# Spreading the scan input of a Mamba layer over its states: one fp32 product on 32 rows instead of three stacked bf16 parts

## The chip, the cores and the metric

One NeuronCore of a Trainium2 chip runs the whole program in one launch. The time is device microseconds (us) of that core, from a run without a profile; the profile comes from one more execution. Engines: TensorE (PE), VectorE (DVE), ScalarE (ACT), GpSimd (POOL) and SyncE (SP), which here only issues DMAs.

## What is computed

Two layers over eight sequences of 512 tokens with 128 features. The first layer (attention between 16 heads, a feed-forward part and a normalisation, plus the routing for the second layer's experts) is not touched. The second layer is a Mamba block beside a mixture of experts. Its heart, for each sequence, with 256 channels d and 16 states n:

```
u  = silu(conv(x @ in_proj));  dt = softplus(dt_r @ dt_proj + b);  A = -exp(A_log)
h[d,n](t) = exp(dt[d](t) * A[d,n]) * h[d,n](t-1)  +  dt[d](t) * u[d](t) * B[n](t)
y[d](t)   = sum over n of h[d,n](t) * C[n](t)
out = (y + u*D) * silu(z) @ out_proj,   added to the experts' result and the residual
```

All of it is fp32 in the reference.

## The kernel before

`layer0` runs first, then `layer1`; the change is in `layer1`. There the eight sequences are "batches" b = 1 to 8, and a batch has 32 groups k: a group holds 8 channels by 16 states, one pair on each of the 128 partitions, over 512 time steps. The table `order` gives for group k the channel half s (k // 16), then i, then j, with j the fastest; SEG is 16, the groups of one half.

For each group:

- `spread_du` (TensorE, L1839) copies dt\*u of the 8 channels to the 128 partitions of the group by a product with a 0/1 matrix `spread`. The result is in one of two PSUM buffers `p_du`. It waits until the scan two groups back has released the buffer.
- `inject` (VectorE, L1726) multiplies `p_du` by the repeated B in place.
- `decay` (ScalarE, L1607) makes exp(dt\*A) in place in the tile `decays` (two of its four buffers lie in `slots`), three groups ahead; a DMA (`load_decays`) has brought dt repeated over the states from the DRAM scratch `dt_rows`, one load for each four groups.
- `scan` (VectorE, L1733) is the recurrence over the 512 steps, into one of four buffers `hs`.
- `times_c` (GpSimd, L1471) multiplies by the repeated C, into `hc`.
- `gather_y` (TensorE, L1848) sums over the states, once for four groups: four fp32 products, each into 32 output columns.

The orders are written out by hand: `batch()` of each engine lists what it does at each k, and each engine executes its list in order. TensorE at step k starts with `spread_du(b, k + 1)` and then does what falls due: the projections of the batch after next (`project_u` at k = 22 to 25 with two taps each, `project_z` at 27 and 29), those of the next batch (`x_proj` at 8, `dt_proj` at 10 and 12), `gather_y` at 2, 6, 10 and so on, `out_proj` at 6 and 23, and the experts. A plan has ten expert units for each batch, two of the shared expert and eight tiles of 256 tokens (48 tiles in all, so batches 7 and 8 have none of their own), due at step 10 + 3.2 m for m = 0 to 9. `due(b, k, ahead)` gives the units to be started: the turn of the tile 7 steps ahead, its gate 6, its up 5, its down product at the due step. VectorE has the unit's `half` (L1746) 4 steps ahead, `skip` at 3 and 19, `result` at 8, and the two ends of the softplus (`softplus_cut`, `softplus_end`, L1705 and L1710) at 15 and 16. GpSimd has the expert product `hidden` (L1483), `steps` at 17 and 19, `gate_y`, and from batch 4 on 64 indirect DMAs that fetch expert results (`fetch`, L1507).

The value that is spread has to be exact to fp32. The kernel before gets this with three bf16 parts. `steps` (GpSimd, L1459 and L1463) makes dt and then dt\*u in the tile `dtu`. For each half s of the next batch: ScalarE rounds dt\*u to bf16 (`first_part`, L1594), VectorE subtracts it (`second_rest`, L1715), ScalarE rounds the rest (`second_part`, L1598), VectorE subtracts again (`third_part`, L1720). They stand at k = 19 to 26. Each part is moved by four DMAs of SyncE's queue (`stack`, L1329, at k = 21 to 23 and 25 to 27) from partitions 32c..32c+31 to rows 32i..32i+31 of the tile `block_in`, so that one bf16 product over 96 rows adds the three parts. SyncE's list also holds the loads of expert weights (`wm`, L1309) and rows (`xg`, L1300), and those of the decays (L1358), and it waits in order.

Before batch 1 a prologue does the same for the first batch: dt\*u, parts, stacks, then the loop.

A fp32 product shows in the trace as two matmul instructions, each with a weight load of its own; a bf16 product as one. So L1848 has 512 instructions and L1839 has 256.

Of the kernel before, what the change touches and what calls it, by code (L numbers as in the profile page):

```python
# [17 lines left out]
BF16 = mybir.dt.bfloat16  # L18
# [43 lines left out]
def constants():  # L62
# [11 lines left out]
    spread = np.zeros((3, 32, 4, 128), np.float32)  # L74
# [20 lines left out]
    for i in range(2):  # L95
# [8 lines left out]
        "c_spread": spread.reshape(96, 4, 128),  # L104
# [1007 lines left out]
def layer1(nc, outer, io, moe, out, ident, w_loaded, n_loads, ready1, hold, w):  # L1112
    with ExitStack() as ctx:
# [13 lines left out]
        NB = 3  # L1127
# [4 lines left out]
        spread = sb("spread", [96, 4, 128], BF16)  # L1132
# [14 lines left out]
        dtu = sb("dtu", [128, 2, ST, T])  # L1147
        ez, rz = dtu[:, 0], dtu[:, 1]
# [3 lines left out]
        rest = wz  # L1152
        part = sb("y_part", [128, ST, 3, T], BF16)

        block_in = sb("block_in", [96, NB, 4, T], BF16)
# [41 lines left out]
        part1 = count("y_part1", 2)  # L1197
        rest1 = count("y_rest1", 2)
        part2 = count("y_part2", 2)
        part3 = count("y_part3", 2)  # L1200
        stacked = [count(f"y_stacked{i}", 3 * 4, 16) for i in range(ST)]
# [73 lines left out]
        def _(sp):  # L1275
            start(sp, [*xt_in, *ht_in, bc_out, bc_in, *stacked, *dt_out, *decays_in, *wm_in, *xg_in, *os_out])
# [41 lines left out]
            def stack(b, s, i):  # L1318
                made = (part1, part2, part3)[i]
                if i == 0:  # L1320
                    if s:
                        sp.wait_ge(du_full.sem, du_full.at(b - 1, SEG))
                    else:
                        sp.wait_ge(du_full.sem, du_full.at(b - 2))
                    hold(sp)
                sp.wait_ge(made.sem, made.at(b, s + 1))
                hold(sp)
                for c in range(4):
                    sp.dma_start(block_in[32 * i:32 * i + 32, (2 * b + s) % NB, c], part[32 * c:32 * c + 32, s, i]).then_inc(stacked[s].sem, 16)  # L1329

            def store_dt(b, s):
# [5 lines left out]
                sp.dma_start(dt_d[b % 2, s].rearrange("r (j t) -> j r t", j=4), dtu[:, 0, s]).then_inc(dt_out[s].sem, 16)  # L1337
# [49 lines left out]
            def prologue():  # L1387
                load_ht(1)
                sp.dma_start(hs[0:96, 2], io["c_spread"].rearrange("r i c -> r (i c)")).then_inc(staged, 16)
# [623 lines left out]
```

## Time and profile before

| | us |
|---|---|
| runs without a profile (3) | 1251.82, 1258.43, 1283.87; median 1258.43 |
| profiled execution, its time | 1268.29 |
| profiled execution, its span | 1266.5 |
| TensorE busy with matmuls | 856.6 (68%) |
| VectorE busy | 934.0 (74%) |
| GpSimd busy | 722.6 (57%) |
| ScalarE busy | 509.3 (40%) |
| first and last scan of layer 1 start at | 544.0 and 1247.3 |
| mean granted TensorE clock | 0.813 of full speed |

The shares of busy time are means over two different layers. The first layer ends at about 500 us; the scans fill the stretch from 544 us to the end but for the last 20 us. The times of runs without a profile scatter by 2.5% here, more than their distance to the profiled execution.

### The profile page before, as it was taken

The page shows a single profiled execution, that of the slowest core. Times are in us where ns is not written, and L with a number is a line of the kernel's source. Part 1 is how long each engine was busy: PE and PEld are TensorE (multiplying, and loading weights), DVE is VectorE, ACT ScalarE, POOL GpSimd, SP SyncE. Part 2 cuts the span into 40 slices and gives each one's busy share as a digit, 9 for nine tenths or more (in the row PEclk, how much of TensorE's full clock was granted, in tenths as well). Part 3 has the DMA queues.
Part 4 walks back from the last instruction along what each step waited for, and adds up shares of the span by engine and source line. Part 5 has one row for each costly group of instructions (what it writes and reads, how often), then busy time and mean ns, then how long its engine had stood idle before and what let it go on. Part 6 is the DMA issues. An engine that isn't in the chain of part 4 may idle for free. (4 is left out here: it accounts for less than half of the span.)

```text
span 1266.5 us, 13006 instructions
## 1 busy us (share of the span) xinstructions
PE 856.6 (68%) x3620; PEld 407.2 (32%) x3620; DVE 934.0 (74%) x1280; ACT 509.3 (40%) x842; POOL 722.6 (57%) x555
## 2 busy tenths in 40 slices
PE   3667888878855717347887878757778777834543
PEld 1123333333322312114544435424444444411210
DVE  3567887798785540176898798859989898969773
ACT  1012312322211103246576585664684574742330
POOL 1022112112106517455778677749998898679996
PEclk9668978998958757767998988978999888955755
DMA  4986666664702123366675766765776777645641
GB/s 126 217 176 154 152 173 174 152 182 109 160 32 83 59 93 121 84 160 198 162 216 178 180 215 167 198 188 125 182 206 162 189 207 173 204 119 112 135 121 29
DMA packets 102835, 192.32 MB, mean 152 GB/s; under 512 B 13131, under 2 KB 68108, under 8 KB 90348
## 3 DMA queue, kind: packets, MB, share of 16 engines
q1 hardware_dynamic: 91500, 183.07, 54.2%
q0 software_dynamic: 11264, 8.43, 3.8%
q8 instruction: 29, 0.48, 0.2%
q14 instruction: 42, 0.34, 0.1%
HBM read 146.80 MB, written 32.06 MB: 141 GB/s over the span
## 5 line engine op out<-in xcount | busy, mean ns | idle before, releaser
L1471 POOL TENSOR_TENSOR hc<-hs,c_rep 128x512 f32<-128x512 f32 x256 | 377.4, 1591 | 114.1 <-DVE hs L1733 113.7
L1726 DVE TENSOR_TENSOR p_du<-p_du,b_rep 128x512 f32<-128x512 f32 x256 | 175.2, 684 | 62.4 <-PE p_du L1839 62.0
L1839 PE MATMUL p_du<-block_in,spread 96*128 96x512 bf16 x256 | 111.4, 441 | 126.8 <-DVE hs L1733 119.5
L1733 DVE TENSOR_TENSOR_SCAN hs<-slots,p_du 128x512 f32<-128x512 f32 x128 | 156.2, 1220 | 40.6 <-POOL hc L1471 27.0
L1733 DVE TENSOR_TENSOR_SCAN hs<-decays,p_du 128x512 f32<-128x512 f32 x128 | 156.2, 1220 | 14.0 <-POOL hc L1471 3.0
L1507 POOL DMA_INDIRECT y_xr<-moe_sums,position x64 | 108.5, 1696 | 39.2 <-issue 25.1
L447 POOL TENSOR_TENSOR sc<-ex,ex_part 128x1024 f32<-128x1024 f32 x8 | 17.0, 2127 | 187.3 <-ACT ex_part L546 187.3
L682 DVE TENSOR_TENSOR value_prod<-p_eb,v 128x512 f32<-128x512 f32 x128 | 83.6, 684 | 37.4 <-PE p_eb L963 37.1
L1607 ACT ACTIVATE decays<-decays,a_neg 128x512 f32<-128x512 f32 x128 | 87.7, 716 | 49.5 <-DMA decays<-dt_rows 49.2
L1848 PE MATMUL p_y<-hc,gather 128*32 128x512 f32 x512 | 83.7, 732 | 35.0 <-POOL hc L1471 35.0
L1839 PEld LDWEIGHTS p_du<-block_in,spread 96*128 96x128 bf16 x256 | 25.4, 100 | 246.2 <-DVE hs L1733 200.8
L1483 POOL TENSOR_TENSOR y_hid<-y_hid,g_in 128x512 f32<-128x512 f32 x64 | 98.3, 1536 | 2.3 <-DVE y_hid L1746 2.3
L1607 ACT ACTIVATE slots<-slots,a_neg 128x512 f32<-128x512 f32 x128 | 89.7, 723 | 24.4 <-DMA slots<-dt_rows 24.4
L1811 PE MATMUL y_misc<-y_ht,wtap 128*128 128x512 f32 x128 | 74.3, 716 | 36.2 <-ACT ur L1550 20.7
L1868 PE MATMUL p_g<-xgt,wm 128*128 128x256 f32 x192 | 61.3, 448 | 47.1 <-ACT xgt L1613 28.6
L1619 ACT ACTIVATE g_in<-p_g 128x512 f32<-128x512 f32 x64 | 38.1, 595 | 112.3 <-PE p_g L1868 87.5
L658 DVE TENSOR_TENSOR score_prod<-qb,p_k 128x2048 f32<-128x2048 f32 x32 | 72.4, 2282 | 12.4 <-issue 6.9
L1895 PEld LDWEIGHTS p_o<-wm,y_hid 128*128 128x128 f32 x384 | 59.5, 225 | 12.7 <-issue 10.8
L1895 PE MATMUL p_o<-wm,y_hid 128*128 128x128 f32 x384 | 59.6, 307 | 0.9 <-ACT os L1626 0.9
L1868 PEld LDWEIGHTS p_g<-xgt,wm 128*128 128x128 f32 x192 | 39.5, 220 | 60.7 <-issue 35.1
L927 PE MATMUL p_s<-score_prod,sum_d 128*32 128x512 f32 x256 | 46.3, 805 | 17.4 <-DVE score_prod L658 17.4
L464 POOL TENSOR_TENSOR root<-var,half 128x8 f32<-128x8 f32 x8 | 13.2, 1648 | 73.2 <-DVE var L731 73.2
(184 smaller groups left out, 1666.2 us busy)
## 6 DMA issues: line engine op xcount, KB each, us to landing
qb<-rq_rows SPq DMA_DIRECT2D x32, 1024.0 KB, 14.1
decays<-dt_rows SPq DMA_DIRECT2D x32, 1024.0 KB
slots<-dt_rows SPq DMA_DIRECT2D x32, 1024.0 KB
wm<-in_wmoe SPq DMA_DIRECT2D x48, 384.0 KB, 13.8
moe_rows<-zeros SPq DMA_DIRECT2D x8, 774.0 KB, 6.3
xg<-moe_rows SPq DMA_DIRECT2D x48, 129.0 KB, 13.7
stack<-ex_part SPq DMA_DIRECT2D x96, 64.0 KB
block_in<-y_part SPq DMA_DIRECT2D x192, 32.0 KB, 5.8
```

The lines of the kernel that those rows point to most:

```text
L682: nc.vector.tensor_tensor(value_prod[:, n % NP], p_eb[:, n % 2], v[:, b % NV], ALU.mult).then_inc(weighed.sem, 1)
L1471: nc.gpsimd.tensor_tensor(hc[:, k % NA], hs[:, k % 4], c_rep[:, p], ALU.mult).then_inc(hc_done.sem, 1)
L1483: nc.gpsimd.tensor_tensor(hid[:, v % 2], hid[:, v % 2], g_in[:, v % 2], ALU.mult).then_inc(hid_done.sem, 1)
L1507: nc.gpsimd.indirect_dma_start(xr[:, b - 1, t], None, moe["sums"][grp], bass.IndirectOffsetOnAxis(ap=position[:, grp, kk, TT * i + t:TT * ...
L1607: nc.scalar.activation(decay_of, decay_of, ACT.Exp, scale=a_neg[:, g:g + 1]).then_inc(da_done.sem, 1)
L1726: nc.vector.tensor_tensor(p_du[:, k % 2], p_du[:, k % 2], b_rep[:, p], ALU.mult).then_inc(dbu_done.sem, 1)
L1733: nc.vector.tensor_tensor_scan(hs[:, k % 4], decays[(8 * (b - 1) + k // 4) % NQ][:, bass.ts(j, T)], p_du[:, k % 2], 0.0, ALU.mult, ALU.add ...
L1811: ins = nc.tensor.matmul(p_misc[:], wtap[:, k, bass.ts(n, 128)], ht[:, b % 2, k:k + T], start=(k == 0), stop=(k == CONV - 1))
L1839: nc.tensor.matmul(p_du[:, k % 2], spread[:, i], block_in[:, (2 * b + s) % NB, j], start=True, stop=True).then_inc(du_full.sem, 1)
L1848: ins = nc.tensor.matmul(p_y[32 * j:32 * j + 32], w["gather"][:, i], hc[:, k % NA], start=(i == 0), stop=(i == 3))
L1868: ins = nc.tensor.matmul(p_g[:, bass.ts(f, 256)], wm[:, j % NR, bass.ts(f, 128)], xgt[:, j % 2], start=True, stop=True)
L1895: ins = nc.tensor.matmul(p_o[:, bass.ts(i, 128)], hid[:, v % 2, 256 * f + 128 * i:256 * f + 128 * i + 128], wm[:, j % NR, 2 * FF1 + 128 * ...
```

## The change

The three parts, their stacks, the tiles `y_part` and `block_in` and all their semaphores go. `spread` becomes an fp32 matrix that stands four times, once for each block of 32 partitions, and TensorE multiplies the 32 partitions of the block j of dt\*u, where they lie, by it. `dtu` is split into `dt`, `rz` and a double-buffered `du`, so that dt\*u of the next batch can stand beside that of this one.

```diff
-        spread = sb("spread", [96, 4, 128], BF16)
+        spread = sb("spread", [128, 4, 128])
-        dtu = sb("dtu", [128, 2, ST, T])
-        ez, rz = dtu[:, 0], dtu[:, 1]
+        dt = sb("dt", [128, ST, T])
+        du = sb("du", [128, 2, ST, T])
+        rz = sb("rz", [128, ST, T])
+        ez = dt[:]
-        part = sb("y_part", [128, ST, 3, T], BF16)
-        block_in = sb("block_in", [96, NB, 4, T], BF16)
...
             def spread_du(b, k):
                 s, j, i = order[k]
                 if k % SEG == 0:
-                    pe.wait_ge(stacked[s].sem, stacked[s].at(b))
+                    pe.wait_ge(dt_step.sem, dt_step.at(b, 2 * s + 2))
                 pe.wait_ge(scanned.sem, ...)
-                nc.tensor.matmul(p_du[:, k % 2], spread[:, i], block_in[:, (2 * b + s) % NB, j], start=True, stop=True)
+                nc.tensor.matmul(p_du[:, k % 2], spread[32 * j:32 * j + 32, i], du[32 * j:32 * j + 32, (b - 1) % 2, s], start=True, stop=True)
...
-                nc.gpsimd.tensor_tensor(dtu[:, 1, s], dtu[:, 0, s], u[:, p, s], ALU.mult)
+                    pool.wait_ge(du_full.sem, du_full.at(b - 2))
+                nc.gpsimd.tensor_tensor(du[:, p, s], dt[:, s], u[:, p, s], ALU.mult)
...
-            def stack(b, s, i):             # SyncE
-            def first_part(b, s):           # ScalarE, L1594
-            def second_part(b, s):          # ScalarE, L1598
-            def second_rest(b, s):          # VectorE, L1715
-            def third_part(b, s):           # VectorE, L1720
...
             # SyncE, prologue
-                load_decays(1, 0)
-                for i in range(3):
-                    stack(1, 0, i)
-                for q in (1, 2):
+                for q in range(3):
                     load_decays(1, q)
-                for i in range(3):
-                    stack(1, 1, i)
```

The waits on `part3` in `dt_in` and `one_more` become one wait on `dt_step`. In the prologue the load of `spread` goes straight into its tile, without the conversion to bf16 on VectorE (L1698). Everything else, and the place of every other step, stays.

## Rows read from the trace of the kernel before

**Rows 1.** Stretches from first scan to first scan of batches 1 to 8, all engines.
```profile
544.00:634.30 90.30, 66.74 (x264) 35.43 (x265) 70.77 (x81) 52.63 (x91) 59.49 (x46) 0.81 0.68 177
634.30:719.80 85.50, 66.57 (x308) 38.35 (x307) 72.56 (x83) 55.12 (x99) 63.20 (x49) 0.92 0.68 189
719.80:804.90 85.10, 67.77 (x310) 39.26 (x309) 72.71 (x83) 55.34 (x100) 63.25 (x49) 0.90 0.68 190
804.90:903.10 98.20, 68.04 (x314) 38.85 (x313) 82.57 (x84) 55.46 (x100) 74.40 (x57) 0.90 0.66 169
903.10:994.90 91.80, 69.67 (x307) 39.99 (x306) 80.08 (x83) 55.41 (x99) 82.78 (x62) 0.89 0.72 184
994.90:1081.70 86.80, 67.55 (x310) 39.32 (x309) 78.65 (x84) 55.42 (x100) 81.46 (x61) 0.90 0.72 191
1081.70:1170.30 88.60, 46.79 (x176) 17.48 (x174) 75.24 (x76) 40.71 (x64) 69.61 (x52) 0.67 0.53 145
1170.30:1247.00 76.70, 38.32 (x126) 12.16 (x126) 60.11 (x67) 20.08 (x32) 73.68 (x54) 0.63 0.49 111
```
**Rows 2.** Timeline: a scan on VectorE and the inject after it.
```profile
545.90 1.22 DVE L1733 TENSOR_TENSOR_SCAN hs<-decays,p_du 128x512 f32<-128x512 f32 x1
...
547.04 0.67 DVE L1726 TENSOR_TENSOR p_du<-p_du,b_rep 128x512 f32<-128x512 f32 x1
```
**Rows 3.** What VectorE waited for, 544 to 1248 us: total, times, longest.
```profile
DVE p_du L1726 <- PE p_du L1839: 44.5, 28, 9.1
DVE hs L1733 <- POOL hc L1471: 30.1, 16, 11.8
```
**Rows 4.** Groups by line from 400 us on, VectorE: busy, mean ns, idle before.
```profile
L1715 DVE TENSOR_TENSOR conv<-dtu,y_part 128x512 f32<-128x512 f32 x16 | 27.5, 1718 | 17.4 <-ACT y_part L1594 17.4
L1720 DVE TENSOR_TENSOR y_part<-conv,y_part 128x512 bf16<-128x512 f32 x16 | 20.3, 1269 | 0.1
```
**Rows 5.** Timeline: one subtraction in batch 4, while GpSimd works.
```profile
874.25 5.42 DVE L1720 TENSOR_TENSOR y_part<-conv,y_part 128x512 bf16<-128x512 f32 x1
```
**Rows 6.** Timeline: SyncE's stacks at the end of batch 2 and what follows.
```profile
708.71 4.98 SPq L1329 DMA_DIRECT2D block_in<-y_part  x8
...
711.80 2.08 PE L1868 MATMUL p_g<-xgt,wm 128*128 128x256 f32 x4 [3.08 <-DMA wm<-in_wmoe]
...
716.52 0.70 DVE L1726 TENSOR_TENSOR p_du<-p_du,b_rep 128x512 f32<-128x512 f32 x1 [3.85 <-PE p_du L1839]
```
**Rows 7.** Timeline: end of the prologue.
```profile
538.66 2.56 ACT L1607 ACTIVATE decays<-decays,a_neg 128x512 f32<-128x512 f32 x4 [1.03 <-DMA decays<-dt_rows]
...
542.56 1.03 PE L1839 MATMUL p_du<-block_in,spread 96*128 96x512 bf16 x2 [6.93 <-DMA block_in<-y_part]
```
**Rows 8.** Timeline, TensorE alone: products in a stream at full clock.
```profile
694.37 1.88 PE L1811 MATMUL y_misc<-y_ht,wtap 128*128 128x512 f32 x4
696.10 1.05 PE L1903 MATMUL p_acc<-wo,yt 128*128 128x128 f32 x8
696.98 0.38 PE L1839 MATMUL p_du<-block_in,spread 96*128 96x512 bf16 x1
```
**Rows 9.** The same, around a gather; the next row starts where it ends.
```profile
658.65 1.07 PE L1848 MATMUL p_y<-hc,gather 128*32 128x512 f32 x8
659.65 0.39 PE L1839 MATMUL p_du<-block_in,spread 96*128 96x512 bf16 x1
659.88 0.81 PE L1878 MATMUL p_u<-xgt,wm 128*128 128x256 f32 x3
```
**Rows 10.** Timeline: a product on 64 rows between products on 128.
```profile
656.51 0.29 PEld L1832 LDWEIGHTS y_misc<-xd,wdt 64*128 64x128 f32 x2 [0.33 <-issue]
656.51 1.12 PE L1832 MATMUL y_misc<-xd,wdt 64*128 64x512 f32 x2
...
657.57 0.97 PEld L1888 LDWEIGHTS p_acc<-shared_w,y_hid 128*128 128x128 f32 x8 [0.76 <-issue]
657.57 1.16 PE L1888 MATMUL p_acc<-shared_w,y_hid 128*128 128x128 f32 x8
```
**Rows 11.** Timeline: the same 64-row product at half clock, after idle time.
```profile
496.17 2.07 PE L1832 MATMUL y_misc<-xd,wdt 64*128 64x512 f32 x2 [0.68 <-ACT xd L1550]
```

More of the change, by code:

```diff
@@ L72, in constants @@
     ident = np.eye(128, dtype=np.float32)
-    spread = np.zeros((3, 32, 4, 128), np.float32)
+    spread = np.zeros((4, 32, 4, 128), np.float32)
     for i in range(4):
@@ L103, in constants @@
         "c_ident": ident,
-        "c_spread": spread.reshape(96, 4, 128),
+        "c_spread": spread.reshape(128, 4, 128),
         "c_gather": gather,
@@ L1126, in layer1 @@
         NO = 3
-        NB = 3
         NQ = 4
@@ L1196, in layer1 @@
         dt_step = count("dt_step", 4)
[L1197 to L1201, printed above, removed]
         dt_out = [count(f"dt_out{i}", 1, 16) for i in range(ST)]
@@ L1275, in _ @@
         def _(sp):
[L1276 removed]
+            start(sp, [*xt_in, *ht_in, bc_out, bc_in, *dt_out, *decays_in, *wm_in, *xg_in, *os_out])
             sp.wait_ge(ready1, 2)
@@ L1316, in store_tile @@
                     .then_inc(os_out[j % NO].sem, 16)
-            def stack(b, s, i):
[L1319 to L1329, printed above, removed]
             def store_dt(b, s):
@@ L1571, in dt_in @@
                 if s == 0:
-                    act.wait_ge(part3.sem, part3.at(b - 1))
+                    act.wait_ge(dt_step.sem, dt_step.at(b - 1))
                 nc.scalar.activation(rz[:, s], p_misc[:], ACT.Relu, bias=w["dt_b"][:, s:s + 1])
@@ L1589, in log_in @@
                 nc.scalar.activation(az, wz, ACT.Ln).then_inc(sp_ln.sem, 1)
-            def first_part(b, s):
-                act.wait_ge(dt_step.sem, dt_step.at(b, 2 * s + 2))
-                act.wait_ge(stacked[s].sem, stacked[s].at(b - 1))
-                nc.scalar.activation(part[:, s, 0], dtu[:, 1, s], ACT.Copy).then_inc(part1.sem, 1)
-            def second_part(b, s):
-                act.wait_ge(rest1.sem, rest1.at(b, s + 1))
-                nc.scalar.activation(part[:, s, 1], rest[:, s], ACT.Copy).then_inc(part2.sem, 1)
             def decay(b, k):
@@ L1640, in prologue @@
                 log_in(1)
-                for s in range(ST):
-                    first_part(1, s)
-                for s in range(ST):
-                    second_part(1, s)
                 for s in range(ST):
@@ L1759, in prologue @@
                 softplus_end(1)
-                for s in range(ST):
-                    second_rest(1, s)
-                for s in range(ST):
-                    third_part(1, s)
             def batch(b, p, old, new, nxt):
@@ L1836, in spread_du @@
                 if k % SEG == 0:
-                    pe.wait_ge(stacked[s].sem, stacked[s].at(b))
+                    pe.wait_ge(dt_step.sem, dt_step.at(b, 2 * s + 2))
                 pe.wait_ge(scanned.sem, scanned.at(b, k - 1) if k >= 2 else scanned.at(b - 1, GROUPS - 1 + k))
-                nc.tensor.matmul(p_du[:, k % 2], spread[:, i], block_in[:, (2 * b + s) % NB, j], start=True, stop=True).then_inc(du_full.sem, 1)
+                nc.tensor.matmul(p_du[:, k % 2], spread[32 * j:32 * j + 32, i], du[32 * j:32 * j + 32, (b - 1) % 2, s], start=True, stop=True).then_inc(du_full.sem, 1)
             def gather_y(b, q):
```

41 lines of the change are left out of this document (10 added, 31 removed).

## Prediction

> **What bounds the kernel now.** I read the second layer alone, batch by batch, because the first is not touched and the two have different limits. The stretches [rows 1] are 77 to 98 us long for 32 groups. The least step of a group is on VectorE: a scan of 1.22 us and an inject of 0.68 us (with the small gaps between them, 1.90 us from inject to inject) [rows 2]. So 32 groups need 61 us, and the other VectorE work of a batch brings it to 71 to 83 us busy [rows 1]. VectorE is the bound: it has 10 to 15 us free in a stretch. Its waits show where these go: 44.5 us for the spread on TensorE in 28 waits, 30.1 us for GpSimd [rows 3]. GpSimd is close behind in batches 5, 6 and 8 (83, 81 and 74 us). TensorE is busy for 67 us in a stretch with experts, but that busy time counts the tail of each product; what matters below is how long it holds the engine, from its start to the next start.
>
> **What goes.** On VectorE 32 subtractions, 27.5 + 20.3 = 47.8 us [rows 4]. Four of them stand in the prologue at about 0.7 us each (2.8 us), so 45.0 us stand in the loop, on the bounding engine. Their mean (1.72 and 1.27 us) is far over the 0.67 us of an inject of the same size, because some lie long beside GpSimd's work; the worst took 5.42 us [rows 5]. Part of such a stretch is GpSimd's own backlog, which stays: I count 42 us as won, with 28 x 0.7 = 20 us as the low end and 45 as the high one. On ScalarE 32 roundings go; it is at 20 to 55 us of each stretch [rows 1], so this is worth nothing, and if ScalarE's lead of three groups were gone it would be worth some 0.6 us each.
>
> On SyncE 24 DMA issues go for each batch, at 0.6 us each (8 of them 4.98 us) [rows 6]. Behind them in this queue the expert weights come late: TensorE waited 3.08 us for them and VectorE then 3.85 us for the spread [rows 6]. This is part of the 44.5 us; I do not count it twice.
>
> In the prologue TensorE waits for the stacks until 542.56, while the first decays are there at 538.66 [rows 7]. dt\*u is then long made, so the new spread is early, and the load of the decays is late next. First scan 4.5 us sooner, between 0 (the three loads of decays now share the DMA engines) and 8.
>
> **What comes: TensorE.** The spread was one bf16 instruction that holds TensorE for 659.88 - 659.65 = 0.23 us [rows 9]. It becomes an fp32 product of two instructions on 32 rows. The trace before has no product on 32 rows, so I bound it. Lower bound: fp32 products on all 128 rows in a stream, 694.37 to 696.10 for two, 0.865 us each [rows 8]. The nearest row is the product on 64 rows [rows 10]: it starts at 656.51 and the next at 657.57, which is 1.06 us. Its weight load is not pulled ahead (idle 0.33 us before it, 0.76 us before the next one's), where the loads of a stream are hidden. The eight instructions after it take 1.16 us and not the 1.05 us of the same form in a stream [rows 8], 0.11 us more, and the product itself starts about 0.09 us late. That makes 1.25 us. I take 1.25 us, the price of the nearest row, so 1.02 us more for each of 256 groups; upper bound 2.07 us, what the same 64-row product took where it ran at 1.2 instead of 2.4 GHz [rows 11] (nearly twice the 1.12 us of [rows 10]).
>
> The Trainium skill, TensorEngine Tiling (Array Packing), Key Properties, says that a change of the tiling mode drains the engine, and lists 64 and 32 rows as modes of their own. The trace agrees by the two uncovered loads around the 64-row product; the bf16 product on 96 rows shows none, its follower starts after 0.23 us [rows 9]. By the rule a spread costs the 1.25 us above; did it not hold for 32 rows, the 0.87 us of rival A.
>
> Now the load of TensorE for one full batch at full clock, by starts. The 16 fp32 products of 512 columns (8 of `project_u`, 2 `project_z`, 2 of `x_proj`, 4 of the shared expert) are 16 x 0.865 = 13.8. Gate and up of eight tiles, the same columns in four instructions each, 16 x 0.86 = 13.8. Twelve groups of eight short products (down, `out_proj`) at 696.98 - 696.10 = 0.88 are 10.6 [rows 8]. Eight turns at 0.22 are 1.8, two `dt_proj` at 1.06 are 2.1 [rows 10], eight gathers at 659.65 - 658.65 = 1.00 are 8.0 [rows 9]. Sum 50.1 us. With the old spreads (32 x 0.23 = 7.4) it is 57.5, well under 85; with the new ones (32 x 1.25 = 40.0) it is 90.1 us, more than the whole stretch has now. **TensorE becomes the bound** in batches with experts.
>
> It is also uneven, and `p_du` has two buffers, so TensorE can be early by only one group. I set its load against VectorE's for each step k of the written order. Steps 22 to 30 hold `project_u`, `project_z`, two gathers beside `out_proj` and nearly three units: 5.1, 4.7, 3.8, 3.2, 4.0, 3.0, 1.5, 3.9, 3.1 = 32.3 us on TensorE against 9 x 1.90 + 3 x 0.66 = 19.1 on VectorE: 13 us late. Steps 6 to 12 (`x_proj`, `dt_proj`, `out_proj`) 21 against 16: 5 late. Steps 0 to 5 lose 1; 13 to 21 are even. So VectorE waits 19 us for the spread in a full batch. Check on batches 2 and 3: VectorE without waits and without the subtractions needs about 74.5 us, plus 19 is 93.6, a little over the 90.1 of TensorE's own load.
>
> **Sum.** Waits on TensorE now, removed to be replaced: -44.5. Subtractions: -42. Prologue: -4.5. New waits: batch 1 has no work of a batch before it and starts its units later: 15. Batches 2 and 3: 19 each. Batches 4 to 6 have part of the lateness under their waits for GpSimd: 15, 18, 18. Batch 7 has no tiles of its own and no `project_u`, batch 8 almost nothing but spreads and gathers; but the granted clock is 0.67 and 0.63 there [rows 1], so 6 and 7.5. Together +117.5. Net +26.5 us. The profiled execution (1268.3) would become 1294.8; it lay 9.9 us over the median of the runs shown, so from the median 1258.4 I forecast **1285 us**, 2.1% slower.
>
> The new wait of the spread for `dt_step` comes at k = 31 for work done by GpSimd at 17 and 19: nothing. The wait of `du` for the spreads two batches back: nothing. Batch b+1's second half is due 14 groups later still.
>
> **The rivals.**
>
> *A: the mode costs nothing, and the VectorE time decides (faster).* If a 32-row product is as cheap as a stream's 0.87 us, the load is 50.1 + 27.8 = 77.9 us and the waits of a full batch fall from 19 to about 10. Then -44.5 - 42 - 4.5 + (8 + 5 x 10 + 3 + 3 = 64) = -27, that is 1231 us. For it: nothing in the trace shows 32 rows. Against: the uncovered loads at 64 rows [rows 10]. Between -27 at 0.87 us and +26.5 at 1.25 us the sum is zero near 1.06 us a spread; below that this side wins. Chance 0.15. The Trainium skill, TensorE: Matmul & The Clock Gate, The mechanism, adds that products on different row groups run side by side, and neighbours here do have different j; but each new spread waits for a scan, so two stand together only seldom.
>
> *B: no change that can be told.* The load is as I say, but GpSimd's waits in batches 4 to 8 cover much more of it, and the weights come earlier because SyncE is free. Waits of 10 in each of batches 4 to 6 (-21) leave +5: 1264 us. For it: GpSimd has 70 to 83 us in these stretches [rows 1]. Against: TensorE is in order and stands still with them. Chance 0.20.
>
> *C: the clock adds to it.* At 1.2 GHz a spread takes 2.07 us and more [rows 11], over the 1.90 us of the VectorE step, so even with nothing beside it each group is late. Batches 7 and 8 have a load of about 63 and 55 us at full clock; at the granted 0.67 and 0.63 that is 94 and 87, 181 us, against the 164 us that they have in my sum: +17. If batches 2 and 3 keep their 0.92 and 0.90 too, 90.1 us become 98 to 100 against 93.6: +11 for the two. 1313 us. For it: the clock in [rows 1]. Against: TensorE will be far busier there, and the stretches where it is busy have 0.9. Chance 0.23.
>
> That leaves 0.42 for my forecast, own range 1270 to 1300. A measurement of this kernel tells apart about 2%, 1233 to 1284. Of the forecast some six tenths lie above it: slower 0.25 + 0.23 = 0.48; faster, nearly all of A, 0.13; the rest 0.39. The range of eight in ten goes from near A to beyond C: 1238 to 1330.
>
> **What would show it.** The new L1839 has 512 matmul instructions, some 1.1 us for a pair at full clock, with a weight load uncovered before it and another before its follower. Subtractions and L1329 are gone, VectorE has about 48 us less busy time. VectorE's wait for `p_du` rises from 44.5 to over 100 us, in steps 23 to 31 and 11 to 13 above all; stretches 2 and 3 are 91 to 96 us; batch 7 gets shorter; the clock is near 1 in batches 2 to 6. The first scan starts near 539.5. I am wrong if the spread holds TensorE for under 1 us, if full stretches stay under 87 us, or if the loss sits in batches 7 and 8.

## The result, and the profile after

The changed kernel takes 1356.7 us (median of 4 runs, 1345.7 to 1360.8) against 1271.1 for the kernel before on the same chip: 1.080 times as long, with a 95% interval of 1.067 to 1.092. (The ratio is of fast executions alone: two of the four of before, both at 1283.9 us, were in a slower state, and are in its median but not in the ratio.) I forecast 1285 us, 2.1% slower, with a range up to 1330. The direction was right, the size was not: the loss is almost four times the forecast one. Its profiled execution took 1354.4 us, 86.1 more than the profiled one of before.

The stretches from first scan to first scan of the eight batches, with the same columns as [rows 1]: length, busy time of TensorE, its weight loads, VectorE, ScalarE and GpSimd, granted clock of TensorE, DMA share, GB/s.

```profile
532.10:646.30 114.20, 110.35 (x292) 45.80 (x292) 70.10 (x77) 51.92 (x90) 58.98 (x46) 0.73 0.53 144
646.30:741.40 95.10, 91.82 (x342) 42.86 (x340) 70.27 (x80) 53.05 (x96) 61.95 (x49) 0.96 0.64 160
741.40:848.00 106.60, 103.33 (x341) 47.03 (x340) 70.98 (x79) 53.03 (x96) 62.04 (x49) 0.86 0.59 145
848.00:956.80 108.80, 105.83 (x341) 47.56 (x340) 74.73 (x79) 53.17 (x96) 74.52 (x57) 0.84 0.63 147
956.80:1052.00 95.20, 91.92 (x342) 42.87 (x340) 70.33 (x80) 53.11 (x96) 80.13 (x61) 0.96 0.69 159
1052.00:1158.60 106.60, 103.33 (x341) 47.06 (x340) 70.95 (x79) 53.01 (x96) 80.13 (x61) 0.86 0.62 162
1158.60:1250.40 91.80, 74.30 (x210) 25.36 (x208) 71.10 (x72) 41.35 (x64) 72.02 (x54) 0.68 0.54 126
1250.40:1340.20 89.80, 78.60 (x164) 23.80 (x164) 62.64 (x68) 17.06 (x28) 75.91 (x55) 0.50 0.39 78
```

TensorE's busy time is now all but 3 to 4 us of every stretch with experts: it has taken over from VectorE as the bound. The clock column is the second thing to see. Batches 2 and 5 have 0.96 and take 95.1 us; batches 3 and 6 do the same work at 0.86 and take 106.6. Batches 1 and 4 are slower still at 0.73 and 0.84, and batch 8, with little but spreads and gathers, stays at 0.50 (that is 1.2 GHz of 2.4) throughout.

What VectorE waited for from 532 to 1341 us, as in [rows 3] (total, times, longest):

```profile
DVE p_du L1668 <- PE p_du L1773: 202.2, 138, 4.9
...
DVE hs L1675 <- POOL hc L1442: 9.4, 4, 5.2
```

The balance of the loop closes with these rows. The wait for the spread went from 44.5 us in 28 waits to 202.2 in 138, +157.7. The scan's wait for GpSimd went from 30.1 to 9.4, -20.7. VectorE's own busy time over the eight stretches fell from 592.7 [rows 1] to 561.1, -31.6 and not the 42 to 48 that I had counted (both are sums of the fourth column). The net is +105.4 (the last window of [rows 1] ends 1.5 us before the last scan does), and the loop took 103.6 us more (808.1, the sum of the lengths, against 704.5 up to the end of the last scan). Before the loop 11.9 us were won (first scan at 532.1, not 544.0), after it 5.8 (12.2 us from the last scan to the end, not 18.0): 103.6 - 11.9 - 5.8 = 85.9, of the 86.1 above.

What TensorE waited for in the loop, first before (544 to 1248 us), then after (544 to 1341 us):

```profile
PE p_du L1839 <- DVE hs L1733: 119.5, 100, 5.6
...
PE p_g L1868 <- DMA wm<-in_wmoe: 18.3, 8, 4.9
```
```profile
PE p_du L1773 <- DVE hs L1675: 24.2, 11, 4.5
PE p_g L1802 <- ACT xgt L1574: 15.5, 5, 3.3
```

TensorE used to wait 119.5 us for a scan to release a buffer; now it is VectorE that waits. The waits for expert weights are gone.

The spread itself, in batch 2 at full clock, TensorE alone (start, duration; each row starts when the one before lets go of the engine), then the weight loads of the same products. These answer to [rows 9, 10].

```profile
663.48 1.12 PE L1773 MATMUL p_du<-du,spread 32*128 32x512 f32 x2
664.53 1.13 PE L1797 MATMUL p_g<-y_xt,shared_w 128*128 128x512 f32 x2
665.59 1.12 PE L1773 MATMUL p_du<-du,spread 32*128 32x512 f32 x2
```
```profile
664.53 0.30 PEld L1797 LDWEIGHTS p_g<-y_xt,shared_w 128*128 128x128 f32 x2 [0.76 <-issue]
665.58 0.29 PEld L1773 LDWEIGHTS p_du<-du,spread 32*128 32x128 f32 x2 [0.76 <-issue]
```

And in batch 3, where the clock has fallen [rows 11]:

```profile
787.67 2.04 PE L1802 MATMUL p_g<-xgt,wm 128*128 128x256 f32 x4 [3.27 <-ACT xgt L1574]
789.50 1.92 PE L1829 MATMUL p_o<-wm,y_hid 128*128 128x128 f32 x8
791.35 2.07 PE L1773 MATMUL p_du<-du,spread 32*128 32x512 f32 x2
793.35 2.08 PE L1812 MATMUL p_u<-xgt,wm 128*128 128x256 f32 x4
795.36 2.07 PE L1773 MATMUL p_du<-du,spread 32*128 32x512 f32 x2
```

At full clock a spread and the product after it take 665.59 - 663.48 = 2.11 us; a 128-row product alone is 0.865, so the spread costs 1.25 us, the load before it and that of its follower both uncovered. At 1.2 GHz the pair takes 795.36 - 791.35 = 4.01 us. TensorE stood still for 3.27 us in front of 787.67 and the clock was low after that; then it worked back to back, and the clock stayed low until 816.6. In the kernel before the low stretches of batches 2 and 3 lasted 3 to 7 us each; here batches 2 and 5 have one of 6.8 us each, batches 1, 3, 4 and 6 one of 31 to 34 us (batch 1 is also low at its start, until 560.6), and from 1192.1 us to the end all is low. The rise in batch 2 came 6.8 us after the fall, behind a wait and products like those of batch 3:

```profile
692.56 2.04 PE L1802 MATMUL p_g<-xgt,wm 128*128 128x256 f32 x4 [3.28 <-ACT xgt L1574]
```

So even with 32 rows in use the clock sometimes comes back soon. What decides between 6.8 and 31 us these traces do not show.

### The profile page after: what moved, and what is told of

It is laid out like the page before. It is cut to its first block and busy times, and to the rows that moved or that the text cites. A ratio compares the mean times of both kernels' runs of the same rounds, so it can differ in the third digit from the quotient of the medians.

```text
span 1352.4 us, 13135 instructions
## 1 busy us (share of the span) xinstructions
PE 1120.9 (83%) x3876; PEld 467.5 (35%) x3876; DVE 897.9 (66%) x1247; ACT 490.6 (36%) x810; POOL 712.3 (53%) x555
## 5 line engine op out<-in xcount | busy, mean ns | idle before, releaser
L1442 POOL TENSOR_TENSOR hc<-hs,c_rep 128x512 f32<-128x512 f32 x256 | 359.5, 1467 | 222.7 <-DVE hs L1675 222.0
L1773 PE MATMUL p_du<-du,spread 32*128 32x512 f32 x512 | 340.8, 803 | 40.6 <-DVE hs L1675 40.5
L1675 DVE TENSOR_TENSOR_SCAN hs<-decays,p_du 128x512 f32<-128x512 f32 x128 | 156.3, 1221 | 26.1 <-ACT decays L1568 14.1
L1773 PEld LDWEIGHTS p_du<-du,spread 32*128 32x128 f32 x512 | 88.5, 224 | 201.6 <-issue 100.1
L1478 POOL DMA_INDIRECT y_xr<-moe_sums,position x64 | 103.5, 1617 | 31.8 <-issue 18.2
L1454 POOL TENSOR_TENSOR y_hid<-y_hid,g_in 128x512 f32<-128x512 f32 x64 | 91.7, 1432 | 3.3 <-DVE y_hid L1688 3.3
L1745 PE MATMUL y_misc<-y_ht,wtap 128*128 128x512 f32 x128 | 70.5, 685 | 17.5 <-DVE a_neg L1653 14.4
L1802 PE MATMUL p_g<-xgt,wm 128*128 128x256 f32 x192 | 64.3, 465 | 15.5 <-ACT xgt L1574 15.5
L1574 ACT ACTIVATE xgt<-p_g 128x256 f32<-128x256 f32 x48 | 18.3, 381 | 157.5 <-PE p_g L1789 157.5
L1812 PE MATMUL p_u<-xgt,wm 128*128 128x256 f32 x192 | 60.6, 444 | 0.0
```

The lines of the kernel that those rows point to most:

```text
L1442: nc.gpsimd.tensor_tensor(hc[:, k % NA], hs[:, k % 4], c_rep[:, p], ALU.mult).then_inc(hc_done.sem, 1)
L1454: nc.gpsimd.tensor_tensor(hid[:, v % 2], hid[:, v % 2], g_in[:, v % 2], ALU.mult).then_inc(hid_done.sem, 1)
L1478: nc.gpsimd.indirect_dma_start(xr[:, b - 1, t], None, moe["sums"][grp], bass.IndirectOffsetOnAxis(ap=position[:, grp, kk, TT * i + t:TT * ...
L1675: nc.vector.tensor_tensor_scan(hs[:, k % 4], decays[(8 * (b - 1) + k // 4) % NQ][:, bass.ts(j, T)], p_du[:, k % 2], 0.0, ALU.mult, ALU.add ...
L1745: ins = nc.tensor.matmul(p_misc[:], wtap[:, k, bass.ts(n, 128)], ht[:, b % 2, k:k + T], start=(k == 0), stop=(k == CONV - 1))
L1773: nc.tensor.matmul(p_du[:, k % 2], spread[32 * j:32 * j + 32, i], du[32 * j:32 * j + 32, (b - 1) % 2, s], start=True, stop=True).then_inc( ...
```

## The experiments

Twelve kernels. Each ratio is against the kernel before, timed beside it on the same chip. A profile shows one execution: kernel 11, whose loop has the code of before, took 693.8 us from the first scan to the end of the last where before took 704.5, so differences of some 10 us between two profiles are not told apart here. In the diffs an `if` stands on one line with its body, indents are left out, and `...` marks what is cut.

**1. Only the rows: the same fp32 product over all 128 rows.** Sixteen 0/1 matrices, zero outside block j, so that the product reads all of dt\*u and gives the same values.

```diff
...
-matmul(p_du[:, k % 2], spread[32 * j:32 * j + 32, i], du[32 * j:32 * j + 32, (b - 1) % 2, s])
+matmul(p_du[:, k % 2], spread[:, j, i], du[:, (b - 1) % 2, s])
```

> The changed kernel, but the spread is an fp32 product on all 128 rows: sixteen 0/1 matrices whose rows outside block j are zero, and all of dt*u as the moving operand; the values are the same. Theory L (load: a 32-row product in between 128-row products costs two uncovered weight loads, all the rest follows): a spread holds TensorE for 0.87 us instead of 1.25, the waits for p_du fall from 210 us to about 90, granted clock as in the changed kernel; 1270 to 1290 us. Theory C (the 32-row products also keep the granted clock down): the same and the clock of batch 8 rises from 0.50 to over 0.8 and that of batches 1, 3, 4, 6 from 0.73 to 0.86 to over 0.93; 1215 to 1250 us, at or under the kernel before. If neither holds it stays above 1330.

Measured: 1283.7 us, 1.005 of before [1.001, 1.009]. The loss shrank from 8.0% to 0.5% with nothing changed but the rows in use. Batches 2, 3 and 8:

```profile
638.80:727.50 88.70, 83.68 (x341) 45.60 (x341) 69.69 (x79) 53.10 (x96) 62.08 (x49) 0.96 0.62 177
727.50:818.00 90.50, 83.43 (x341) 44.94 (x341) 69.70 (x80) 53.27 (x96) 62.16 (x49) 0.98 0.65 159
1173.80:1252.50 78.70, 54.96 (x165) 19.10 (x164) 60.89 (x68) 18.82 (x31) 75.53 (x56) 0.88 0.44 97
```

Batch 8 has as many instructions and a clock of 0.88 where it had 0.50. And the wait for `xgt` that preceded the fall in batch 3 is there as well, but the clock is back after 6.8 us (TensorE alone; the products from 687.02 on get shorter):

```profile
681.76 2.05 PE L1807 MATMUL p_g<-xgt,wm 128*128 128x256 f32 x4 [4.00 <-ACT xgt L1579]
683.60 1.92 PE L1834 MATMUL p_o<-wm,y_hid 128*128 128x128 f32 x8
685.31 1.91 PE L1778 MATMUL p_du<-du,spread 128*128 128x512 f32 x2
687.02 1.22 PE L1817 MATMUL p_u<-xgt,wm 128*128 128x256 f32 x4
```

The time lies where the theory of the load put it, the clock where that of the clock did: with 128 rows both the hold (0.86) and the clock change, so one more run is needed to part them (7).

**2. One bf16 pass on 32 rows.** dt\*u and the matrices in bf16; the low bits of dt\*u are left out.

```diff
-spread = sb("spread", [128, 4, 128])
-du = sb("du", [128, 2, ST, T])
+spread = sb("spread", [128, 4, 128], BF16)
+du = sb("du", [128, 2, ST, T], BF16)
...
```

> The changed kernel with dt*u and the 0/1 matrices in bf16: one instruction on 32 rows in place of two (the low bits of dt*u are left out). It separates the change of rows from the second pass. Theory L: the spread holds TensorE for about 0.23 + 0.4 = 0.6 us at full clock, load 70 us in a full batch, hardly any wait for p_du: 1220 us. Theory C: the clock in batches 7 and 8 is low, but so is the load; the same. If the row change costs nothing the pair of starts is 0.23 us apart and the time 1205.

Measured: 1262.0 us in one run, beside 1278.3 for before; one run gives no interval. That is some 40 us over what I expected; VectorE still waits 79.6 us for the spread in 43 waits. A spread and the following product take 1.38 us here (662.75 to 664.12), so the hold is about 0.5 us. What became of the missing gain is the question of experiment 4.

**3. The product alone, nothing removed.** The kernel before, with the 32-row fp32 product, which reads `u` in place of dt\*u (the factor dt is left out). Parts, subtractions and stacks all stay. As in the change, `spread` is loaded straight into its tile, so this kernel also has the earlier sends of experiment 11.

```diff
...
-matmul(p_du[:, k % 2], spread[:, i], block_in[:, (2 * b + s) % NB, j])
+matmul(p_du[:, k % 2], spread[32 * j:32 * j + 32, i], u[32 * j:32 * j + 32, (b - 1) % 2, s])
```

> The kernel before with all of its parts, subtractions and stacks, but the spread is the 32-row fp32 product of the changed kernel, on the tile u (dt is left out of the scan's input, the work is the same). It prices the TensorE part by itself. From the changed kernel (+86 us) and a saving of 47 us for what went: about 1400 us if the two parts simply add; 1360 us or less if the removed VectorE work would lie under the new waits for TensorE anyway, so that the removal is worth nothing once TensorE is late. I expect the latter mostly: 1370.

Measured: 1368.7 us, 1.065 [1.052, 1.079]. Its batches 2 and 3:

```profile
658.50:765.00 106.50, 103.22 (x342) 46.99 (x340) 73.96 (x84) 55.16 (x100) 63.27 (x49) 0.86 0.57 155
765.00:860.00 95.00, 91.64 (x341) 42.80 (x340) 73.18 (x83) 55.15 (x100) 63.24 (x49) 0.96 0.64 165
```

95.0 us at 0.96 and 106.5 at 0.86: to a tenth the stretches of the changed kernel at the same clocks, though VectorE works 3 us more in each. In the stretch at 0.96 it waits 16.1 us for the spread, where the changed kernel's batches 2 and 5 have 20.3 each; at 0.86 it is 26.6 against 30.6 in batch 3. What VectorE no longer had to do, it waited instead. With TensorE as the bound the subtractions cost nothing in these stretches, so their removal brings nothing.

**4. The removal alone.** The changed kernel with a bf16 product over 96 rows of a constant tile, as cheap as the old one; the spread of dt\*u is left out. The conversion of `spread` to bf16 is there, but GpSimd's sends do not wait for it.

```diff
...
-matmul(p_du[:, k % 2], spread[32 * j:32 * j + 32, i], du[32 * j:32 * j + 32, (b - 1) % 2, s])
+matmul(p_du[:, k % 2], spread[:, i], block_in[:, j])
```

> The changed kernel with the bf16 product on 96 rows of the kernel before, on a constant tile (the spread of dt*u is left out; TensorE's work is that of before). It prices the removal by itself. My prediction's terms: 42 us of subtractions, 4.5 us of prologue and some of the 44.5 us of waits for weights that came late: 1195 to 1215 us.

Measured: 1258.6 us, 0.983 [0.974, 0.992]. That is a gain of some 22 us, well short of the expected one. By the profile 9.9 us of it are in the prologue (the first scan starts 69.2 us after GpSimd's first memset of the layer, 79.0 before); the loop went from 704.5 to 688.7, but beside the 693.8 of kernel 11 that is only 5.1 us. VectorE's wait for the spread, 547 to 1237 us:

```profile
DVE p_du L1672 <- PE p_du L1777: 68.6, 40, 9.6
```

And what TensorE waited for in the same kernel, 545 to 1340 us, with the longest such wait, at the end of batch 5:

```profile
PE p_g L1806 <- DMA wm<-in_wmoe: 22.8, 6, 7.6
...
979.92 2.08 PE L1806 MATMUL p_g<-xgt,wm 128*128 128x256 f32 x4 [7.57 <-DMA wm<-in_wmoe]
```

The wait for the spread rose from 44.5 to 68.6 although the spread is as cheap as ever. The subtractions stood at k = 20 to 26, beside `project_u`; without them VectorE reaches the next spread sooner and waits there (0.2 to 1.9 us at k = 24, 25 and 28), and at k = 31 it waits 3.2 to 9.6 us in five of the batches. The 9.6 us stand behind TensorE's wait for expert weights above. These weights come late although the stacks are gone: 22.8 us of waits in 6, where before had 18.3 in 8 and kernel 11, with the stacks, 7.2 in 5. Kernel 2 has 13.3 us of such waits too. So of the 45 us in the loop even the old bound gives back only 5 us (profile against that of kernel 11) to 16 (against that of before; the ratios 0.983 and 0.996 of kernels 4 and 11 are also 16 us apart, and their intervals leave some 13 us either way).

**5. Streams by themselves.** At the head of the program, fp32 products of 512 columns back to back, 24 of each kind: on 128 rows (L1037), 32 (L1039), 64 (L1041), 128 (L1043), 64 (L1045), on four blocks of 32 in turn (L1047), then twelve pairs of 128 rows and 32 (L1049, L1050). It was run once; its total time holds these streams and is not compared.

```diff
+            for n in range(24):
+                nc.tensor.matmul(p_eb[:, 0], *rows_stream(128, 0), start=True, stop=True)
+            for n in range(24):
+                nc.tensor.matmul(p_eb[:, 0], *rows_stream(32, 0), start=True, stop=True)
...
+            for n in range(24):
+                nc.tensor.matmul((p_eb, p_s)[n % 4 // 2][:, n % 2], *rows_stream(32, 32 * (n % 4)), start=True, stop=True)
+            for n in range(12):
+                nc.tensor.matmul(p_a1[:], *rows_stream(128, 0), start=True, stop=True)
+                nc.tensor.matmul((p_eb, p_s)[n % 4 // 2][:, n % 2], *rows_stream(32, 32 * (n % 4)), start=True, stop=True)
```

> The changed kernel with streams of fp32 products of 512 columns ahead of layer 1's first product, 24 of each, without a wait: 128 rows, 32 rows (one block), 64 rows, 128, 64, 32 rows (the four blocks in turn, four PSUM banks), and last 12 pairs of a 128-row and a 32-row product. It adds some 200 us at the start. Theory C: the granted clock is 1.0 in the 128-row streams and falls to 0.5 in the 32-row stream although TensorE never idles; 0.865 us a product at 128 rows, 1.7 us at 32 rows. Theory L alone: the clock stays at 1.0 in all of them, 0.865 us a product in every stream, 1.25 us more for each 32-row product of the pairs. The skill's page TensorE: Matmul & The Clock Gate would have the four blocks in turn run side by side, some 3 times as fast as one block.

Windows cut where the stream or the clock changes (L1037, L1039 in two, L1041, L1043 in two, L1045), columns as above:

```profile
14.60:36.80 22.20, 22.18 (x48) 9.59 (x48) 2.55 (x14) 0.00 (x0) 2.29 (x2) 1.00 0.08 22
36.80:41.60 4.80, 4.80 (x12) 2.14 (x12) 0.00 (x0) 0.00 (x0) 0.00 (x0) 0.98 0.00 0
41.60:73.60 32.00, 32.00 (x38) 11.99 (x36) 0.00 (x0) 0.00 (x0) 0.00 (x0) 0.50 0.00 1
73.60:114.90 41.30, 41.30 (x50) 15.85 (x49) 0.00 (x0) 0.00 (x0) 0.00 (x0) 0.50 0.00 0
114.90:120.00 5.10, 5.10 (x7) 2.15 (x7) 0.00 (x0) 0.00 (x0) 0.00 (x0) 0.51 0.00 0
120.00:138.10 18.10, 18.10 (x43) 7.79 (x41) 0.00 (x0) 0.00 (x0) 0.00 (x0) 1.00 0.00 0
138.10:159.00 20.90, 20.90 (x53) 8.97 (x52) 0.00 (x0) 0.00 (x0) 0.00 (x0) 1.00 0.00 1
```

TensorE is busy in every microsecond of these rows. The stream on 128 rows runs at 1.00. The one on 32 rows falls to 0.50 while it never pauses and stays there. The stream on 64 rows that follows stays at 0.50 for 41 us; that on 128 rows comes back to 1.00; and the same 64-row stream behind it keeps 1.00 for its 21 us. So here 128 rows brought the full clock back, 64 held it but did not bring it back, and 32 did not hold it. Then the pairs, at full clock:

```profile
164.29 1.12 PE L1049 MATMUL p_a<-rope,wq 128*128 128x512 f32 x2
165.34 1.12 PE L1050 MATMUL p_eb<-rope,wq 32*128 32x512 f32 x2
166.40 1.12 PE L1049 MATMUL p_a<-rope,wq 128*128 128x512 f32 x2
```

2.11 us a pair, less the 0.86 between two starts in the streams of 128 rows: 1.25 us for the 32-row product, as I had it from the 64-row one [rows 10]. In this even mixture the clock held at 1.00.

**6. Sixty-four rows.** Eight matrices, half the partitions of dt\*u.

```diff
-matmul(p_du[:, k % 2], spread[32 * j:32 * j + 32, i], du[32 * j:32 * j + 32, (b - 1) % 2, s])
+matmul(p_du[:, k % 2], spread[64 * (j // 2):64 * (j // 2) + 64, j % 2, i], du[64 * (j // 2):64 * (j // 2) + 64, (b - 1) % 2, s])
```

> The changed kernel, the spread on 64 rows (eight 0/1 matrices, zero rows for the other block). The row change is there as in the changed kernel, so theory L has the same 1.25 us and 1350 us. Theory C: if twice the rows hold the clock up better, batch 8 is over 0.5 and the time lies between the changed kernel and the 128-row one, 1300 to 1330 us.

Measured: 1338.2 us, 1.061 [1.055, 1.068]. By its total it is not told from the 32-row kernels, which have 1.052 (10), 1.065 (3) and 1.080 (the change). In batch 8 it lies between: a clock of 0.65 and 79.7 us, where the three 32-row kernels have 0.50 to 0.56 and 85 to 90 us and kernel 1 has 0.88 and 78.7. Full stretches take 99 to 106 us. The hold is that of 32 rows (662.43 to 664.54 for it and its follower, 2.11 us).

**7. The load without the clock.** Kernel 1 with a product of 232 columns ahead of each spread into the same buffer, which the spread overwrites, so that the pair holds TensorE for 1.25 us with 128 rows in use.

```diff
+matmul(p_du[:, k % 2, 0:232], spread[:, j, i], du[:, (b - 1) % 2, s, 0:232])
 matmul(p_du[:, k % 2], spread[:, j, i], du[:, (b - 1) % 2, s])
```

> The 128-row fp32 product, and ahead of it in the same PSUM buffer a second one of 232 columns whose result is overwritten, so that a spread holds TensorE for 0.86 + 0.39 = 1.25 us at full clock, as the 32-row product does, but all on 128 rows. It separates load from clock. Theory C (the load of 1.25 us makes full stretches of 95 us, and the rest of the loss of the changed kernel is time at 1.2 GHz that only the 32-row products allow): full stretches 93 to 97 us, none with a granted clock under 0.93, batch 8 over 0.85 and near 80 us; 1290 to 1310 us, near what was predicted for the changed kernel. Theory L2 (the load alone, whatever the rows, gives the loss): like the changed kernel, 1340 to 1360 us, with stretches of 106 us again.

Measured: 1315.4 us, 1.033 [1.025, 1.040]. The hold is right (662.37 to 663.62, 1.25 us) and the clock stays up, batches 2 and 8:

```profile
645.00:741.80 96.80, 93.97 (x405) 57.61 (x404) 70.53 (x80) 53.03 (x96) 62.06 (x49) 0.98 0.67 152
1220.50:1298.10 77.60, 59.56 (x226) 27.36 (x224) 61.05 (x68) 18.86 (x31) 74.42 (x56) 0.99 0.45 98
```

Full stretches take 95.1 to 96.8 us but for batch 4 (104.3). In batch 8 of the change TensorE was the busier, 78.6 us of 89.8, and had 0.50; here it is busy for 59.6 of 77.6 us and has 0.99. So it is not idle time that keeps the clock down there.

This run divides the loss: 3.3% comes with the load of 1.25 us a spread (less what the removal and the prologue give), and what lies between it and 1.080, a factor of 1.046 or about 58 us, goes with the 32 rows and the clock that they do not hold. The two ratios are from different chips, and their intervals leave 1.03 to 1.06; from kernels 3 and 10, also on 32 rows, the factor would be 1.03 and 1.02. That there is such a part is shown, its size is not fixed.

**8. An evener order.** Kernel 1 with TensorE's projections spread more evenly over the steps, and what follows them on the other engines moved along.

```diff
...
-if 22 <= k <= 25: project_u(b + 2, (k - 22) // 2, ((0, 1), (2, 3))[(k - 22) % 2])
-if k in (27, 29): project_z(b + 2, (k - 27) // 2)
-if k in (10, 12): dt_proj(b + 1, (k - 10) // 2)
+taps_at = {15: (0, (0, 1)), 17: (0, (2,)), 18: (0, (3,)), 20: (1, (0,)), 21: (1, (1,)), 24: (1, (2,)), 25: (1, (3,))}
+for n, taps in [taps_at[k]] if k in taps_at else []: project_u(b + 2, n, taps)
+if k in (28, 31): project_z(b + 2, (k - 28) // 3)
+if k in (11, 12): dt_proj(b + 1, k - 11)
```

> The 128-row kernel with project_u moved from k = 22 to 25 to k = 15, 17, 18, 20, 21, 24, 25 (one or two taps each), project_z to 28 and 31, dt_proj to 11 and 12. If the waits for p_du at k = 12 and 24 to 28 (about 8 us of a full stretch) come from the uneven order alone, six full stretches get 5 to 7 us shorter: 1240 to 1250 us. If the total load of TensorE is what counts, it changes by less than 5 us.

Measured: 1280.2 us, 1.003 [0.999, 1.008]: no gain over kernel 1 that can be told. The waits only moved, to k = 14, 15 and 18, where TensorE waits for ScalarE's transposed rows; one of 10.3 us stands at k = 31 of batch 5, where TensorE waits 7.5 us for expert weights.

**9. The same, with the softplus one step later.** ScalarE's logarithm, `softplus_end`, `steps` and `store_dt` each one step later.

```diff
-if k in (18, 20): store_dt(b + 1, (k - 18) // 2)
+if k in (19, 21): store_dt(b + 1, (k - 19) // 2)
-if nxt and k in (17, 19): steps(b + 1, q, (k - 17) // 2)
+if nxt and k in (18, 20): steps(b + 1, q, (k - 18) // 2)
...
```

> The same, and ScalarE's logarithm of the softplus one step later, behind the copy of the turned tile for which TensorE waits 4 us in each full stretch (softplus_end, steps and store_dt one step later too). If that wait is the ACT chain's, VectorE's 4 us wait at k = 18 goes: another 3 us in each of six stretches, 1220 to 1235 us, faster than the kernel before by over 2%.

Measured: 1285.5 us, 1.010 [1.006, 1.013], slower than before by 1% where I had expected a gain of over 2%. The wait at k = 18 is gone, and 5 to 11 us appear at k = 31 in batches 3 to 6: `store_dt` now stands later in SyncE's queue, which executes in order, and the expert weights behind it land late. From 725 to 1107 us this queue waits 50.0 us for ScalarE's `os` and 37.8 for GpSimd's `dt`, and TensorE 31.8 us for the weights.

**10. The softplus one step later in the changed kernel.** The edit of 9 in the kernel of the change, to take away the idle time after which the clock fell in batch 3.

> The changed kernel (32 rows) with only the logarithm one step later. In it each low-clock stretch of a full batch begins in TensorE's wait for ScalarE at k = 16 and ends in the project_u stream about 31 us later. Theory C, second part (32-row products do not bring a clock back that an idle stretch took): without the idle time the clock stays at 1.0 in the full batches, stretches 3, 4 and 6 fall from 107 to 92 to 95 us, 1300 to 1320 us. If the clock falls by itself under 32-row products, the low stretches stay and it is 1340 or more.

Measured: 1346.7 us, 1.052 [1.038, 1.066]: not the 1300 to 1320 us that I expected if the idle time were the cause. Batches 2 and 3:

```profile
653.40:753.50 100.10, 99.39 (x341) 46.09 (x340) 70.97 (x79) 52.91 (x96) 61.98 (x49) 0.90 0.62 159
753.50:845.60 92.10, 89.96 (x341) 41.23 (x340) 70.19 (x79) 52.99 (x96) 61.99 (x49) 1.00 0.67 152
```

Batch 3 kept 1.00 and took 92.1 us, but in batch 2 the clock fell at 705.7 all the same, behind 0.71 us of idle time, in a stretch where nearly every second product is a spread:

```profile
702.06 1.12 PE L1774 MATMUL p_du<-du,spread 32*128 32x512 f32 x2
...
704.89 1.28 PE L1774 MATMUL p_du<-du,spread 32*128 32x512 f32 x2 [0.71 <-DVE hs L1676]
...
708.43 2.07 PE L1774 MATMUL p_du<-du,spread 32*128 32x512 f32 x2
```

So a long idle stretch is not needed; in experiment 5 the clock fell with none at all. Which mixture of rows falls and which holds (the pairs of experiment 5 held for 25 us) these runs do not settle.

**11. The sends alone.** A side effect that I had overlooked. In the kernel before, GpSimd's 32 sends of the prologue waited for VectorE's conversion of `spread` to bf16, and that for a DMA; the change took the conversion away. Here the kernel before, with the conversion signalling another semaphore, so that only TensorE waits for it.

```diff
-pool.wait_ge(begun, 3)
+pool.wait_ge(begun, 2)
...
-nc.vector.tensor_copy(spread[...], hs[0:96, 2]).then_inc(begun, 1)
+nc.vector.tensor_copy(spread[...], hs[0:96, 2]).then_inc(tapped, 1)
...
```

> The kernel before, but GpSimd no longer waits for VectorE's conversion of spread to bf16 ahead of its 32 sends (the conversion signals another semaphore). In the changed kernel this side effect of the edit let the sends start 9 us sooner after GpSimd's first instruction, and the first scan came 12 us sooner. If that wait carries the gain of the prologue: the sends 9 us sooner, the first scan 8 to 9 us sooner, 0.6 to 0.7% faster. If the stacks were what mattered, as my prediction had it, nothing changes.

The waits of the kernel before from 440 to 544 us had it:

```profile
POOL moe_rows L1491 <- DVE spread L1698: 8.7, 1, 8.7
DVE spread L1698 <- DMA wtap<-in_taps: 8.7, 1, 8.7
```

GpSimd's memset and first send, in the changed kernel:

```profile
464.06 0.10 POOL L1421 MEMSET y_ht<- 128x6 f32 x1 [16.04 <-POOLq L167]
464.95 1.03 POOL L1462 DMA_INDIRECT moe_rows<-slots,position  x1 [0.79 <-ACT a_neg L1515]
```

Measured: 1271.2 us (12 runs), 0.996 [0.991, 1.001]. The first send starts 1.0 us after the memset (0.9 in the changed kernel) in place of 8.8, and the first scan 69.2 us after it in place of 79.0 (68.0 in the changed kernel), though the stacks are all there. Over the whole run the gain of 0.4% is just not told from none.

**12. Earlier sends and an evener order.** Kernel 11 with `project_u` and `project_z` moved as in 8.

> The same with project_u at k = 15, 17, 18, 20, 21, 24, 25 and project_z at 28 and 31. In the kernel before TensorE is not the bound, so its uneven order should matter little: another 0 to 5 us, 0.5 to 1.1% faster than the kernel before in all. If SyncE's queue and the weights are upset by it, it is slower than the one beside it.

Measured: 1267.0 us (12 runs), 0.994 [0.990, 0.998]. It beats both kernels, by a little: 0.6%. Whether the evener order adds to kernel 11's gain is not told apart.

## Why the prediction was wrong, point by point

Put by what one spread holds TensorE for, the kernels without the subtractions give one row:

| hold of a spread | rows | clock of batch 8 | ratio to before |
|---|---|---|---|
| 0.23 us (4) | 96, bf16 | 0.61 | 0.983 |
| 0.86 us (1) | 128 | 0.88 | 1.005 |
| 1.25 us (7) | 128 | 0.99 | 1.033 |
| 1.25 us at full clock (the change) | 32 | 0.50 | 1.080 |

**The bound changes to TensorE: right**, by its busy time and by who now waits for whom. **The price of 1.25 us: right**, by the starts in the kernel and by the pairs of experiment 5.

**The load of a full batch: right, at the clock that it assumed.** I had 93.6 us. Batch 3 of kernel 10, at 1.00, took 92.1; batches 2 and 5 of the change, at 0.96, took 95.1. By steps, batch 2 waited 5.5 us up to k = 12 (I had 6), 10.2 from k = 24 on (13 for 22 to 30), and 3.6 at k = 18, where I had none: TensorE stood there for ScalarE's `xgt`.

**The term that failed: "Together +117.5" for the new waits, because it took full clock for granted.** It is 202.2. VectorE's waits for the spread by the batch of the spread (the first batch's counted from 532 us on), with the clock of the stretch:

| batch | 1 | 2 | 3 | 4 | 5 | 6 | 7 | 8 |
|---|---|---|---|---|---|---|---|---|
| forecast | 15 | 19 | 19 | 15 | 18 | 18 | 6 | 7.5 |
| measured | 37.3 | 20.3 | 30.7 | 24.9 | 20.4 | 31.1 | 12.2 | 25.7 |
| clock | 0.73 | 0.96 | 0.86 | 0.84 | 0.96 | 0.86 | 0.68 | 0.50 |

The two batches at 0.96 are within 3 us of the forecast, and 81 of the 85 us of excess lie in the others: 22 in batch 1, 18 in batch 8, 12 and 13 in batches 3 and 6, 10 in batch 4, 6 in batch 7. A full batch alone, at 1.00, 0.96 and 0.86 of the clock, takes 92.1, 95.1 and 106.6 us. I wrote "the clock is near 1 in batches 2 to 6" and, against rival C, "the stretches where it is busy have 0.9". But the busy stretches of before were busy with products on 96 and 128 rows, all but two `dt_proj` a batch. Nothing in my working asked what the clock depends on besides busy time. Rival C, with 0.23 and 1313 us, named the clock, though not the rows. Its 181 us for batches 7 and 8 came true (91.8 + 89.8), and so nearly did its +11 for batches 2 and 3, though not as it thought: it left them 0.92 and 0.90, and they have 0.96 and 0.86 and took 14.5 us more than my two times 93.6. What it left out is batches 1, 4 and 6, at 0.73 to 0.86. Of the signs that I named, "batch 7 gets shorter" and "the clock is near 1 in batches 2 to 6" failed: batch 7 took 91.8 us for 88.6, and only the stretches of batches 2 and 5 have 0.96.

The Trainium skill, TensorE: Matmul & The Clock Gate, What's actually happening, says that TensorE is throttled by default and that its activity releases the throttle. The runs agree in part: the stretches of before with the fewest products have 0.67 and 0.63 [rows 1]. But in experiment 5 TensorE had been busy without a pause since 14.6 us when its clock fell to half at 41.6, with 32 rows in use, so being busy is not all that counts.

**"I count 42 us as won" for the subtractions: wrong.** Beside the new bound they were worth nothing (experiment 3), on the old one 5 to 16 us (experiment 4). In the full batches I had checked against TensorE's own load, but the sum still took 42 us off. The same error is in rival A, the case on the other side: at 0.87 us a spread I gave 1231 us, with VectorE waiting 64 us. Kernel 1 has this price, a clock of 0.93 to 0.98 in the full batches, and waits of 101 us; its ratio is 1.005. So the sum is zero not at 1.06 us a spread but below 0.86: on a straight line between kernels 4 and 1 near 0.7, an estimate.

**The size of the load by itself.** Kernel 7 has it: 3.3%, about 41 us, where I had 26.5. This part of the miss is just within my own range (1258.4 us and 41 are 1299); the rows and their clock made the rest.

**The prologue and the end.** "First scan 4.5 us sooner" became 11.9, of which 0.9 lie before the layer's first memset. The load of the decays was late next, as written: the first scan now waits 14.1 us for a decay, and that for its DMA. But the stacks were not what mattered: kernel 11, which keeps them, starts its first scan 9.8 us sooner after the memset, of the 11.0 of the change, by the sends alone. I had costed at nothing the conversion that the diff deletes, without naming who waited for it, and a row of the waits named it. The 5.8 us at the end were not in the sum either, nor the 20.7 us less that the scan waits for GpSimd, which rival B had in part ("-21").

**SyncE's queue: wrong in its cause.** In the changed kernel the weights come in time, but not because the stacks are gone: kernel 4 has no stacks either, and TensorE waits 22.8 us for weights there, where before has 18.3 and kernel 11, which keeps the stacks, 7.2. Kernel 1 has 2.5 us and the change none; that their busier TensorE asks for the weights later would explain it, but no run shows it by itself.

The Trainium skill, TensorEngine Tiling (Array Packing), Key Properties, says that a change of the tiling mode drains TensorE. The trace agrees, with 1.25 us for a 32-row product between 128-row ones against 0.86 for one more of 128 rows.

**What stays open.** Why a mixture of spreads and full products lost the clock in the kernel and kept it in the pairs of experiment 5. That the rows in use count is shown by kernels 1 and 7 beside the change, by batch 8 of kernel 6 and by the streams; at what mixture they do is not. Nor is it known why, behind a like wait, the clock was low for 6.8 us in batches 2 and 5 and for 31 in batches 3 and 6.

## What to carry to other kernels

When a change moves the bound to another engine, price the new bound at the clock that its new instructions can hold, not at that of the stretch before, and count savings on the old bound as nothing until a run shows them. Short-row products are dearer than zero-padded ones twice over here: 1.25 against 0.86 us each, and a clock that often comes back late or not at all; zeros in the other 96 rows took the loss from 8.0% to 0.5%. And when an operation is deleted, look in the list of waits for everyone who waited for it.

## What was not expected of the hardware

The granted clock depends on the rows in use: in streams that never paused it was 0.50 on 32 rows, came back on 128, and on 64 stayed what it had been (experiment 5, 0.50 for 41 us and 1.00 for 21). Products on four different blocks of 32 rows ran side by side: 24 of them in 5.4 us (158.93 to 164.29), 0.22 each, where in the stream on one block each took 0.86 while the clock was full:

```profile
159.46 0.59 PE L1047 MATMUL p_eb<-rope,wq 32*128 32x512 f32 x2
159.47 0.59 PE L1047 MATMUL p_s<-rope,wq 32*128 32x512 f32 x2
```

In this kernel that is of no use, since each spread waits for a scan of its own.
